# Batch 0 of an adapted MoE-LoRA kernel: the gate chain, LoRA-B's difference and the order of the SP queue

## What is computed

```python
x = x + (x @ B0[id].T) @ A0[id].T                       # rank 16
base   = einsum('btd,od->bto', x, W)
logits = x @ Wr.T + 5 * one_hot(language_id)
gates  = scatter(softmax(top_k(logits, 2)))             # b t e
h      = einsum('btd,erd->bter', x, A)
x = x + base + 2 * einsum('bter,bte,eor->bto', h, gates, B)
```

## Time and profile before

| | |
|---|---|
| median of 3 runs | 1561.79 us (1558.64 to 1563.39) |
| the profiled execution | 1558.6 us, span of the core 1556.8 us |
| TensorE busy | 1540.6 us, 99% of the span |
| VectorE busy | 1229.8 us, 79% |
| ScalarE busy | 713.9 us, 46% |
| GpSimd busy | 79.7 us, 5% |
| mean rate of the DMA engines | 223 GB/s |

### The profile page before, as it was taken

The page is one execution under the profiler, slowest core; times in us unless marked ns, Lnnn a source line. Parts: engine busy times, 40 slices in busy tenths (PEclk is TensorE's granted clock), DMA queues, the critical chain, the costliest instruction groups (busy, mean ns, idle before and its releaser), DMA issues.

```text
span 1556.8 us, 20275 instructions
## 1 busy us (share of the span) xinstructions
PE 1540.6 (99%) x7430; PEld 1296.3 (83%) x7430; DVE 1229.8 (79%) x1692; ACT 713.9 (46%) x911; POOL 79.7 (5%) x119
## 2 busy tenths in 40 slices
PE   9989999999999999999999999999999999999998
PEld 9778878888888888888888888888888888888887
DVE  6998878977798768887688776997769976787665
ACT  6522222544445444455445444454444554445442
POOL 2333331000000000000000000000000000000000
PEclk9999999999999999999999999999999999999999
DMA  9899998777777777688676977668777777666664
GB/s 263 222 278 282 269 255 243 223 228 200 228 228 218 213 203 227 215 235 216 209 219 201 255 204 223 215 206 232 207 216 229 214 217 197 213 221 218 197 219 160
DMA packets 303109, 347.04 MB, mean 223 GB/s; under 512 B 204890, under 2 KB 236682, under 8 KB 302346
## 3 DMA queue, kind: packets, MB, share of 16 engines
q1 hardware_dynamic: 293602, 314.28, 70.9%
q0 software_dynamic: 9136, 30.94, 6.0%
q10 hardware_dynamic: 272, 0.52, 0.1%
HBM read 278.52 MB, written 66.72 MB: 222 GB/s over the span
## 4 chain that ended last, share of the span: by engine, by line
PE 94%; DVE 4%; DMA 1%; issue 1%; ACT 0%; POOL 0%; SPq 0%; DVEq 0%; POOLq 0%; ACTq 0%
PE pb L804 28%; PE pb L806 27%; PE pb L805 27%; PE pb L378 5%; PE pb L380 2%; PE pb L533 2%; DVE raw L684 1%; DVE xl L558 1%; PE pb L319 1%; DVE pool_a L540 1%; DMA t_scr<-ost 0%; DMA a0g<-a0p 0%; DVE wl L800 0%; PE pb L1046 0%; PE pb L493 0%
## 5 line engine op out<-in xcount | busy, mean ns | idle before, releaser
L796 ACT CAST wh<-raw 128x1024 fp32r<-128x1024 f32 (+1 forms) x453 | 475.1, 1049 | 702.1 <-PE pb L806 658.7
L800 DVE TENSOR_TENSOR wl<-raw,wh 128x1024 fp32r<-128x1024 f32 (+1 forms) x453 | 551.9, 1218 | 257.8 <-ACT wh L796 256.8
L804 PE MATMUL pb<-wh,sh 128*128 128x512 f32 x1568 | 617.9, 394 | 0.5 <-DVE ost L858 0.5
L806 PE MATMUL pb<-wh,sl 128*128 128x512 f32 x1568 | 611.9, 390 | 0.0
L805 PE MATMUL pb<-wl,sh 128*128 128x512 f32 x1568 | 610.4, 389 | 0.0
L806 PEld LDWEIGHTS pb<-wh,sl 128*128 128x128 f32 x1568 | 294.2, 188 | 64.1
L805 PEld LDWEIGHTS pb<-wl,sh 128*128 128x128 f32 x1568 | 294.9, 188 | 55.7
L804 PEld LDWEIGHTS pb<-wh,sh 128*128 128x128 f32 x1568 | 294.4, 188 | 55.4 <-DVE wl L800 0.9
L378 PE MATMUL pb<-awb,xah 128*128 128x304 f32 x512 | 136.6, 336 | 0.0
L380 PE MATMUL pb<-awb,xal 128*128 128x152 f32 x512 | 119.2, 233 | 0.0
L804 PE MATMUL pb<-wh,xh 128*128 128x512 f32 x256 | 102.4, 400 | 0.7 <-DVE xl L558 0.7
(11 more groups left out here) (153 smaller groups left out, 1257.8 us busy)
## 6 DMA issues: line engine op xcount, KB each, us to landing
raw<-t_scr SPq DMA_DIRECT2D x392, 512.0 KB, 4.1
xst<-in_x_dram SPq DMA_DIRECT2D x448, 64.0 KB, 3.9
out_dram<-ost SPq DMA_DIRECT2D x72, 256.0 KB, 3.8
raw<-in_L_cond_W_dram SPq DMA_DIRECT2D x124, 128.0 KB, 5.0
raw<-bt_scr SPq DMA_DIRECT2D x28, 512.0 KB, 3.7
out_dram<-u SPq DMA_DIRECT2D x56, 256.0 KB, 2.9
t_scr<-raw POOLq DMA_DIRECT2D x32, 256.0 KB, 4.5
t_scr<-tst POOLq DMA_DIRECT2D x16, 512.0 KB, 6.8
```

Source lines behind the costliest of these rows:

```text
L796: e.copy(pair_split(wh, g), pair_source(g)).then_inc(c_wh, 1)
L800: e.tensor_tensor(out=pair_split(wl, g), in0=pair_source(g), in1=pair_split(wh, g).bitcast(f32), op=ALU.subtract).then_inc(c_wl, 1)
L804: e.matmul(o, h, wh[:, g % RING, k, :], start=start, stop=False)
L806: return e.matmul(o, l, wh[:, g % RING, k, :], start=False, stop=stop)
```

## The change

Five edits, all of them to the order of work in batch 0's slots.

1. `gate_weights(0)` and `gated(0)` move on VectorE to directly behind `top_two(0)` in slot 6, ahead of `w_turn(9)`. Before, `w_turn(9)` stood between `top_two` and `gate_weights`, and `gated` was the first work of slot 7.
2. `bt_difference` moves from GpSimd's slot 6 to VectorE's slot 8, behind `pair_lo(10)`; its store stays on GpSimd and moves from slot 6 to slot 8.
3. On VectorE `columns_lo` and `x_lo` of batch 1 come ahead of `w_turn(i + 3)` in slots 9 to 24.
4. On SP `first_load(i + 5)` comes ahead of batch 1's `x_load` in each slot.
5. On SP `adapter_columns(1)` moves from slot 6 to slot 7, there behind `x_load`, and `adapter_rows(1)` from slot 6 to slot 23.

```diff
         def pool_main(e):
...
-                if i == 6:
-                    bt_difference(e)
+                if i == 8:
                     bt_difference_store(e)
...
         def dve_main(e):
             for i in range(SLOTS0):
-                if i == 7:
-                    gated(e, 0)
                 if i == 9:
                     columns_turn(e, 1)
...
                 if i == 6:
                     aux_final(e, 0)
                     top_two(e, 0)
+                    gate_weights(e, 0)
+                    gated(e, 0)
                 if i == 7:
                     hg_lo(e, 0)
+                if i == 8:
+                    bt_difference(e)
...
-                if i + 3 < SLOTS0 and (i + 3) % 9 != 8:
-                    w_turn(e, i + 3)
                 if i == 9:
                     columns_lo(e, 1)
                 if 9 <= i < 25:
                     x_lo(e, 1, i - 9)
+                if i + 3 < SLOTS0 and (i + 3) % 9 != 8:
+                    w_turn(e, i + 3)
                 if i in (17, 25):
                     aux_sum(e, 1, (i - 17) // 8)
                 if i + 2 < SLOTS0 and (i + 2) % 9 != 8:
                     w_sums(e, i + 2)
-                if i == 6:
-                    gate_weights(e, 0)
...
         def sp_main(e):
             for i in range(SLOTS0):
+                if i + 5 < SLOTS0 and i != 3:
+                    first_load(e, i + 5)
                 if 4 <= i < 8:
                     x_load(e, 1, i // 2 - 2, (2, 3) if i % 2 else (0, 1))
                 if 10 <= i < 22:
                     x_load(e, 1, i // 2 - 3, (2, 3) if i % 2 else (0, 1))
-                if i + 5 < SLOTS0 and i != 3:
-                    first_load(e, i + 5)
-                if i == 6:
+                if i == 7:
+                    adapter_columns(e, 1)
+                if i == 23:
                     adapter_rows(e, 1)
-                    adapter_columns(e, 1)
```

## The result

The changed kernel takes 1568.41 us (median of 6 runs, 1566.02 to 1571.95), the kernel before 1560.97 us (6 runs, 1558.23 to 1563.39): ratio 1.0047, 95% interval 1.0030 to 1.0065. It is slower, by 7.4 us in the medians. The forecast was 1565.6 in a range of 1557 to 1570, with slower by over 0.3% at 0.32 and within 0.3% at 0.52. The profiled execution took 1566.02 us with a span of 1564.2 us, 7.4 us over that of before, so the two traces can be laid side by side.

The account below looks back on a forecast made before the run. TensorE, busy for 99% of the span, was taken to bound the kernel. Terms -4.0 (stall) -2.5 (clock) +1.0 (`hg_lo`) +7.0 (columns) +2.5 (clock), less 0.2 rounding, gave +3.8 us: 1565.6 us, range 1557 to 1570.

Parts of the forecast that it names:

- rival 4: SP queue slower than forecast (x at 4.45 us, landings 7 us or more): +8 to +11 us, about 1571; chance 0.13.
- Rival 3: Slot 6's gate instruction stays slow, held by something other than `bt_difference`: +6.7 us, 1568.5; chance 0.06.
- The gate chain: Slot 6 on VectorE: gate instruction 0.19 us, TensorE waits 0.4 instead of 4.4 us without clock drop; -6.5 us.
- The wait for `hgl`: TensorE's `first_gated(8)` waits 1.0 us, as ScalarE takes `pair_hi(9)` before `hg_hi`; the clock is kept.
- LoRA-B's difference on VectorE: The moved `bt_difference` costs VectorE 1.2 us; VectorE reaches `columns_turn(1)` at 109.2.
- The columns on SP: `adapter_columns(1)`, last in slot 7, lands at 115.8; TensorE idles 7.0 us before `aux_products(1, 0)`.
- The clock after it: After TensorE's new stall at `aux_products(1, 0)`, a clock at half speed costs 2.5 us.
- The rest: W ahead of x, `x_lo` ahead of `w_turn`, and `adapter_rows` in slot 23: no further cost.
- Rival 1: Faster: columns land by 109.2, the freed chain keeps its gain; -5.2 us, 1556.6; chance 0.16.

Follow-up runs that it names:

- diff_only: The kernel before with only LoRA-B's difference moved to VectorE; 1565.6 us, ratio 1.0018.
- cols5: The changed kernel with `adapter_columns(1)` in SP's slot 5 instead of 7; 1565.17 us, ratio 1.0029.
- cols6: The changed kernel with `adapter_columns(1)` in SP's slot 6, behind W(11) and x, ahead of W(12); 1568.59 us, ratio 1.0053.
- x_first: The changed kernel with x ahead of W on SP again, columns still last in slot 7; 1561.97 us, ratio 0.9998.
- cols_ahead: The changed kernel with SP's order x, columns (slot 6), W; 1563.02 us, ratio 1.0003.
- x_act: cols_ahead with batch 1's x loads issued by ScalarE's queue instead of SP's, the same bytes; 1554.7 us, ratio 0.9956.
- diff_xlo: The kernel before with only LoRA-B's difference on VectorE and `x_lo` ahead of `w_turn`; 1563.3 us, ratio 1.0008.
- x_act_before: The kernel before with only batch 1's x loads moved to ScalarE's queue; 1560.11 us, ratio 0.9996.
- light_ahead: cols_ahead storing two of the four sums and reloading those for products 4 and 5, whose output is then wrong; 1552.03 us, ratio 0.9931.

## Why the prediction was right, and where it was off

The kernel is slower by the mechanism that was forecast, the late columns, and the measured median lies 1.6 us inside the upper end of a range that was made wide downwards. But the forecast put the change at +3.8 us and the medians have +7.4, and the outcome that was given the most chance, within 0.3% (0.52), did not come. The result lies between the forecast and rival 4, the slower queue (0.13). Rival 3's number, 1568.5, is nearest to the measured one, and that is chance: its cause, a gate instruction that stays slow, is excluded by the 0.19 us at 95.50. Term by term:

**The gate chain** (0.4 us, gate at 0.19, no clock drop): right in each term. diff_only shows the cause of the 3.11 us.

**The wait for `hgl`** (1.0 us): 0.8, and its reason, `pair_hi(9)` ahead of `hg_hi`, is in the trace.

**LoRA-B's difference on VectorE** (1.2 us): 1.22. VectorE reached `columns_turn` at 118.20 - 9.45 = 108.75, forecast 109.2.

**The columns on SP** (7.0 us of idle TensorE): the place, the order and the waiting chain were right, the size was 2.6 us short. W(11) started at 97.87 (98.2), W(12) took 2.18 us (2.64), but the second batch of x 4.28 us where the sum had 2.20, the columns' last issue began 2.86 us into them (2.75), and it landed 118.20 - 111.61 = 6.6 us later (5.6). The last x and the landing carry all of it, +2.1 and +1.0. I had the dear row, 4.45 us at 91.59, and set it aside because GpSimd's stores of LoRA-B fell there. They did not. In the kernel before they were issued beside the x ahead of it:

```profile
82.08 1.50 POOL L1194 DMA_DIRECT2D bt_scr<-bt  x2
82.27 4.47 SPq L292 DMA_DIRECT2D xst<-in_x_dram  x4
```

They landed 7.4 and 8.4 us after their issue, so by about 91.2, and the x at 91.59 took 4.45 us without them. An x at over 4 us stands once more in that trace (4.11 us at 150.83), so the high price was one to be put into the sum. What makes the same four issues take 2.1 or 4.3 us, no run here shows.

**The clock after it** (2.5 us): 3.0. The stretch at half speed was 6.3 instead of 5.6 us. With the 2.6 us above this makes 3.1 of the 3.6 us between +3.8 and +7.4.

**"The rest" at nothing** is the step that failed, though the total does not show it. Of W ahead of x it says that this "shifts x by one batch", and looks at x's first block alone. It did not ask what x itself stands behind, and "After slot 10 TensorE is later than before, so no supply is tighter" took the supply as given: in the changed kernel `x_turn` waits 15.0 us for x in six places (1.0 us before). That TensorE is spared because it is 3.8 us late already and slow for 6 us is what cols5 and cols6 speak for: they take this cover away, and TensorE waits over 5 us in one place. x_first shows W ahead of x to be worth the whole loss, through the columns, which the sum had, and through x, which it had not.

**Rival 1** (faster, from -5.2 us on, had the columns landed by 109.7) named a gain that did not come where its condition was met: in cols5 they landed in time, and the kernel stayed 0.3% slower than before. Its premise, that slots 11 to 28 can run 5 us earlier, holds neither with W ahead of x nor, by cols_ahead, with x ahead on SP's queue.

**The rule weighed against the rows.** The Trainium skill (DMA: Bandwidth & Descriptors, Issuing engines are not separate DMA queues) calls the sequencer's time usually small beside the DMA. The trace disagrees for this case: the x at 104.35, 64 KB a DMA, held SP for 0.45 to 1.58 us an issue, 4.28 us for four, and landed 4.5 to 6.0 us after; and x_act, which changes only the queue that issues x and its place there, goes from the 1.0003 of cols_ahead to 0.9956. That page also says that the engines are shared whatever queue starts a DMA, and that only issue time is saved by a second. The rise from 265 to 280 GB/s does not decide this: no run here tells saved issue time from two queues being served at once.

## What to carry to other kernels

When a load moves behind another in an in-order queue, write down what the other waits for, and follow that engine's list until it either ends or comes back to the load's own consumer: here it came back, and x was a slot late. Before counting on a freed wait, look at how much idle time the queue that feeds the following slots has, and how much will be left. SP's waits for turns between 97 and 233 us were 13.2 us before, 3.6 in cols_ahead, where the gain was returned, and 45 in x_act, where it stood. The 13.2 us looked like enough for a gain of 5 to 7 and were not, so idle time of the queue is a warning and not a budget. And a new stall in place of the one removed takes the clock with it again.

## What was not expected of the hardware

A VectorE instruction of 0.19 us took 3.11 us while GpSimd subtracted 128x1024 f32 in SBUF, and 0.18 to 0.19 in every run without that. By the trace it began 0.7 us before the subtraction, whose span on GpSimd is rough; how the one holds the other is not shown. The issue time of the same DMA (64 KB of x, four at a time) was 2.14 and 4.28 us within 5 us of one another on SP. DMAs issued by ScalarE held up its next work: in x_act the rounding of LoRA-B in slot 6 stood behind four issues of x,

```profile
88.14 3.59 ACTq L292 DMA_DIRECT2D xst<-in_x_dram  x4
91.83 0.62 ACT L796 CAST wh<-bt 128x512 fp32r<-128x512 f32 x1 [3.07 <-issue]
```

VectorE waited 0.57 us for it ahead of `aux_final`, and the wait for `gated` became 1.1 us instead of 0.4. The idle time that costs TensorE its clock has no sharp border in these runs: 1.6 us at `delta(1, 0)`, 2.0 in diff_xlo (slot 10) and 2.2 and 2.3 in cols_ahead (at 192.6 and at `delta(1, 0)`) left it at 2.4 GHz, 1.9 us in cols6, 2.0 in cols5 (at 127.5) and 2.1 in diff_xlo (at `delta(1, 0)`) did not, and all of 2.8 us and more between 90 and 245 us were followed by 1.2 GHz.

Nor are two profiled executions alike ahead of the edits: between 12 and 16 us the granted clock was 0.57 in the changed kernel and 0.69 in the kernel before, but 1.00 in cols_ahead, x_first and x_act_before, and cols_ahead reaches the middle of slot 10 at 110.93 where light_ahead, with the same order, does at 112.13. So steps within a trace can be compared, but ends of two traces only to about 1 us.
